# One more preparation step ahead of layer 0's expert tiles, early row loads, and two sine products moved from GpSimd to VectorE

## The chip, the core and the metric

The kernel runs on one core of a Trainium2 chip. A core has TensorE (PE in the rows; PEld is its weight load), VectorE (DVE), ScalarE (ACT), GpSimd (POOL) and SyncE (SP), each with an instruction queue of its own that runs in order; they wait for each other by semaphores. SyncE does nothing here but issue DMAs. The metric is device microseconds of one execution.

## What is computed

Two layers over a batch of 8 rows (sequences) of 512 tokens with 128 channels. The change is in layer 0, between its first mixing part and its attention scores. Cut to what matters there:

```
xn = layernorm(x)
# attention of layer 0, its preparation per batch row
q_amp = softplus(xn @ Wq_amp.T);  k_amp likewise      # then divided by the head's root mean square
q_phi = pi * tanh(xn @ Wq_phi.T); k_phi likewise
q_cos, q_sin = q_amp * cos(q_phi), q_amp * sin(q_phi) # the same for k
v = xn @ Wv.T
scores = (q_cos . k_cos + q_sin . k_sin) / sqrt(8) * exp(score_log_scale), causal, softmax
# feed-forward of layer 0, after its own small attention y = layernorm(...)
idx = argmax(y @ Wg.T)                                # one of 8 experts per token
out = relu(y @ W1[idx] + b1[idx]) @ W2[idx] + b2[idx]
z = layernorm(y + out) * g2 + be2
```

## The kernel before

The phases setup, mix0, middle0, attend0, middle1, experts1 and attend1 follow each other, each with its own block per engine and a barrier between. The change is in middle0 alone, which does two things side by side.

**Preparation of the attention, one batch row u (0 to 7) after the other.** Row u's 512 x 128 input comes by `load_row`, TensorE transposes it (`turn_row`) and multiplies it with the value, phase and amplitude weights (`values`, `phases`, `amplitudes`, `mean_squares`). ScalarE makes tanh, the softplus out of Abs, Exp and Ln, the sine and the cosine, and the inverse root mean square. VectorE makes |tanh| (`absolute_turn`), the amplitude, its normalised form (`normalise`) and the product with the cosine (`cosine_products`), GpSimd the product with the sine (`sine_products`). VectorE then splits the values into two float16 parts (`split`: a cast and a subtraction), and SyncE stores them to memory as six stacks (`store_stacks`).

**Experts.** At the start VectorE chooses each token's expert (`route_choice`), and GpSimd scatters all 4096 token rows to `sorted0` by expert with 32 indirect DMAs (`scatter`). There are 23 tiles of 256 sorted rows, each with one expert. For tile n SyncE loads the expert's weights and the rows (`load_weights`, `load_rows`; ring of 4 tiles), TensorE transposes the rows (`turn_rows`), projects them in (`into_hidden`) and out (`out_of_hidden`), ScalarE and VectorE each make half of the hidden layer (`half_hidden`), VectorE adds and normalises, GpSimd adds the bias, makes the inverse deviation and applies gain and shift.

What sets the order is one list. A step t has three parts, and each part holds one tile slot, n = 3t + part - FIRST_TILE, with FIRST_TILE = 9; so tiles 0 to 2 are in step 3, and tile 22 is in step 10. Each engine walks this list and does in each part first or last what is due of rows t, t - 1, t - 2 or t - 3 and of tiles n + 1 to n - 3. In step t, TensorE projects row t, ScalarE and VectorE make the amplitude of row t - 1 and normalise row t - 2, and part 0 splits row t - 3. Ahead of the list SyncE loads rows 0 and 1 of the input, waits for the tile table, loads the weights of tiles 0 to 3, then rows 2 and 3, waits until the scatter has landed, and loads the sorted rows of tiles 0 to 3. In the list it stores stacks of row t - 3 and loads row t + 1 in part 0, and loads tile n + 3 in every part. When tile 19 is due it stores the table of the tokens' places, element by element, in eight DMAs (`turn_places`), and when tile 21 is due it waits for these and reads the table back; results of tiles follow in the same queue (`store_result`). GpSimd's queue begins with the scatter, so whatever it does for rows or tiles is behind it.

## Time and profile before

| | us |
|---|---|
| median of 3 runs | 1249.08 |
| lowest and highest of them | 1247.53, 1249.44 |
| the profiled execution, whole | 1250.84 |
| its span in the trace | 1249.3 |
| of that, busy: PE / DVE / ACT / POOL | 990.1 / 835.6 / 680.5 / 638.6 |

The span is that of one execution under the hardware profiler, and the rows further down are from it. A row of a timeline has the start and the duration in microseconds, the engine, the kernel line, the operation, what it writes and reads, how many instructions were merged into it, and in brackets how long the engine had idled before it and what ended that wait. SPq is SyncE's queue issuing a DMA. A row of windows gives each engine's busy time in a stretch, with the number of its instructions, the granted TensorE clock as a share of full speed, the mean busy share of the 16 DMA engines and their GB/s. Layer 0's middle0 lies between about 162 and 387 us.

### The profile page before, as it was taken

What the parts mean: (1) busy time and instruction counts of PE and PEld (TensorE: products, weight loads), DVE (VectorE), ACT (ScalarE), POOL (GpSimd) and SP (SyncE); (2) the same over time, 40 slices, a digit from 0 to 9 for tenths busy, and PEclk for the clock granted to TensorE, in tenths of its full rate; (3) what the DMA queues carried; (4) which work ended last, traced back from release to release, by engine and by line L of the source; (5) the groups of instructions that cost most, each with busy time, mean ns of one, the idle gap of its engine ahead of it and who ended that gap; (6) DMA issues with size and microseconds to landing.
All of it is one profiled execution on the core that took longest, in us unless ns stands there. A gap on an engine that the chain in (4) does not pass through costs nothing. (4 is left out here: it accounts for less than half of the span.)

```text
span 1249.3 us, 25988 instructions
## 1 busy us (share of the span) xinstructions
PE 990.1 (79%) x8908; PEld 647.7 (52%) x8908; DVE 835.6 (67%) x1829; ACT 680.5 (54%) x1293; POOL 638.6 (51%) x908
## 2 busy tenths in 40 slices
PE   3789753989873999999975463499999599999997
PEld 1456431767662555555533342388888245545553
DVE  1566341799986999999937566033333799999992
ACT  1356443777720777777765353122222377777775
POOL 3467537478764454444533456111110467777775
PEclk9899776899996899999997566699999599999999
DMA  4322032477795222222202233466664112211211
GB/s 136 109 50 53 27 101 85 139 212 204 221 144 124 71 78 73 71 70 70 70 8 57 70 109 103 139 191 183 190 193 139 43 43 53 54 53 54 54 47 32
DMA packets 151526, 122.58 MB, mean 98 GB/s; under 512 B 31712, under 2 KB 134032, under 8 KB 151408
## 3 DMA queue, kind: packets, MB, share of 16 engines
q1 hardware_dynamic: 141664, 102.89, 30.2%
q0 software_dynamic: 8016, 17.71, 5.0%
q8 instruction: 67, 1.10, 0.4%
q10 hardware_dynamic: 1728, 0.46, 0.2%
q14 instruction: 51, 0.42, 0.1%
HBM read 75.75 MB, written 42.61 MB: 95 GB/s over the span
## 5 line engine op out<-in xcount | busy, mean ns | idle before, releaser
L2104 ACT ACTIVATE attend_probs<-attend_attend_ps 128x512 f32<-128x512 f32 x640 | 353.8, 601 | 155.3 <-PE attend_attend_ps L2172 144.2
L2071 POOL TENSOR_SCALAR_AFFINE_SELECT attend_probs<-attend_probs 128x512 f32<-128x512 f32 x256 | 159.7, 636 | 194.1 <-ACT attend_probs L2104 193.4
L2172 PE MATMUL attend_attend_ps<-attend_q,attend_ks 50*128 50x512 f16 (+3 forms) x1024 | 235.8, 306 | 22.9 <-ACT attend_probs L2104 20.3
L2140 PE MATMUL attend_attend_ps<-attend_ks,attend_q 48*128 48x512 f16 (+3 forms) x1024 | 191.1, 316 | 30.5 <-DMA attend_ks<-k_stack 22.9
L2185 PE MATMUL attend_attend_ps<-attend_probs,attend_vals 128*32 128x512 f32 (+3 forms) x2048 | 178.3, 445 | 0.0
L2267 DVE TENSOR_REDUCE attend_neg_max<-attend_attend_ps 128x2 f32<-128x1024 f32 x128 | 155.7, 1216 | 13.4 <-PE attend_attend_ps L2152 12.7
L2152 PE MATMUL attend_attend_ps<-identb,stairs 64*128 64x128 bf16 (+1 forms) x1280 | 144.3, 213 | 0.0
L2172 PEld LDWEIGHTS attend_attend_ps<-attend_q,attend_ks 50*128 50x128 f16 x1024 | 70.4, 94 | 119.3 <-ACT attend_probs L2104 72.6
L2269 DVE TENSOR_REDUCE attend_neg_max<-attend_attend_ps 128x2 f32<-128x768 f32 x128 | 121.9, 953 | 7.7 <-PE attend_attend_ps L2152 6.9
L2152 PEld LDWEIGHTS attend_attend_ps<-identb,stairs 64*128 64x128 bf16 x1280 | 104.0, 100 | 19.5 <-issue 4.7
L1887 PE MATMUL experts_experts_ps<-experts_rowsT,experts_w_in 128*128 128x256 f32 (+1 forms) x468 | 110.6, 387 | 1.6 <-ACT experts_rowsT L1836 1.5
L1852 DVE TENSOR_TENSOR experts_hidden<-experts_experts_ps,experts_gate 128x512 f32<-128x512 f32 x39 | 27.0, 692 | 120.7 <-ACT experts_gate L1828 120.7
L1815 POOL DMA_DIRECT2D experts_rows<-sorted x39 | 27.7, 711 | 136.6 <-issue 136.6
L1091 POOL DMA_INDIRECT sorted<-middle_scaled,rank_row x64 | 65.3, 1020 | 59.9 <-issue 38.1
L1887 PEld LDWEIGHTS experts_experts_ps<-experts_rowsT,experts_w_in 128*128 128x128 f32 (+1 forms) x468 | 82.8, 183 | 17.9 <-ACT experts_rowsT L1836 2.1
L2140 PEld LDWEIGHTS attend_attend_ps<-attend_ks,attend_q 48*128 48x128 f16 x1024 | 68.2, 96 | 44.4 <-DMA attend_ks<-k_stack 23.3
L1828 ACT ACTIVATE experts_gate<-experts_experts_ps 128x512 f32<-128x512 f32 x39 | 23.3, 597 | 121.4 <-PE experts_experts_ps L1887 121.4
L2264 DVE TENSOR_REDUCE attend_neg_max<-attend_attend_ps 128x4 f32<-128x1024 f32 x64 | 78.4, 1225 | 9.5 <-PE attend_attend_ps L2152 9.1
L2087 POOL DMA_INDIRECT attend_moe<-done,back_row x64 | 62.1, 970 | 14.9 <-issue 14.9
L1899 PE MATMUL experts_experts_ps<-experts_w_out,experts_hidden 128*128 128x128 f32 (+1 forms) x468 | 58.7, 275 | 0.9 <-DVE experts_result L1863 0.9
L2185 PEld LDWEIGHTS attend_attend_ps<-attend_probs,attend_vals 128*32 128x32 f32 x2048 | 44.7, 108 | 23.9 <-issue 6.4
L1899 PEld LDWEIGHTS experts_experts_ps<-experts_w_out,experts_hidden 128*128 128x128 f32 (+1 forms) x468 | 55.4, 191 | 1.2 <-issue 1.1
(317 smaller groups left out, 1990.4 us busy)
## 6 DMA issues: line engine op xcount, KB each, us to landing
experts_w_in<-in_L_ffn_w_dram SPq DMA_DIRECT2D x78, 176.0 KB, 2.4
q_stack<-middle_parts SPq DMA_DIRECT2D x24, 256.0 KB
k_stack<-middle_parts SPq DMA_DIRECT2D x24, 256.0 KB
attend_q<-q_stack SPq DMA_DIRECT2D x64, 96.0 KB
attend_ks<-k_stack SPq DMA_DIRECT2D x64, 96.0 KB
middle_w_in<-in_L_ffn_W_dram SPq DMA_DIRECT2D x23, 256.0 KB
middle_w_out<-in_L_ffn_W_dram SPq DMA_DIRECT2D x23, 256.0 KB
experts_rows<-sorted POOLq DMA_DIRECT2D x39, 128.0 KB, 2.5
```

The lines of the kernel that those rows point to most:

```text
L1091: pool.indirect_dma_start(k.sorted1, bass.IndirectOffsetOnAxis(ap=k.rank_row[:, c * NT + tile:c * NT + tile + 1], axis=0), scaled[:, c, ti ...
L1887: mm = pe.matmul(ps[0:size[c], hidden_bank(u, bank), half * ROWS:(half + 1) * ROWS], w_in[:, u.phase, w + c * P:w + c * P + size[c]], rows ...
L1899: mm = pe.matmul(ps[:, OUT, a * D:(a + 1) * D], hidden[0:size[c], u.par, c, a * P:(a + 1) * P], w_out[0:size[c], u.phase, c, :], start=(c ...
L2071: pool.affine_select(out=block_, in_=block_, compare_op=ALU.is_ge, fill=0.0, base=0, pattern=[[0, GH], [1, P]], channel_multiplier=-1).the ...
L2104: act.activation(probs[:, u.par, 2 * c + side, :], ps[:, PROB + side, :], ACT.Exp, scale=SCALE ** -2)\
L2140: pe.matmul(ps[:, bank + side, col:col + (qt + 1) * P], q[rows(side, KR), g, pair, qt * P:(qt + 1) * P], ks[rows(side, KR), g, pair, 0:(qt ...
L2152: mm = pe.matmul(span[:, :, col:col + 64], k.stairs[here, stair:stair + P], k.identb[here, here].unsqueeze(1).broadcast_to([64, len(blocks ...
L2172: mm = pe.matmul(ps[:, PROB + side, col:col + S - kt * P], ks[rows(side, KM), g, pair, kt * P:(kt + 1) * P], q[rows(side, KM), g, pair, kt ...
L2185: mm = pe.matmul(ps[32 * h:32 * h + 32, MIX, kt * P:S], vals[:, u.par, kt * GH + h, :], probs[:, u.par, 2 * c + h % 2, col:col + S - kt * ...
L2264: ins = dve.tensor_reduce(out[:, :, :, 1], pair_banks.rearrange("p s (h t) -> p s h t", h=HP), X_AXIS, ALU.max, negate=True)
L2267: ins = dve.tensor_reduce(out[:, :, c // 2, 3], pair_banks, X_AXIS, ALU.max, negate=True)
L2269: dve.tensor_reduce(out[:, :, c // 2, 2], pair_banks[:, :, 0:384], X_AXIS, ALU.max, negate=True)
```

## The change

FIRST_TILE becomes 12, so that each tile meets the row work of one step later, and step 3 has row work and no tile. SyncE's start is written anew: rows 0, 1 and 2 of the input are loaded first, row 3 behind the weights of tile 0, then the weights of tiles 1 to 3. The wait for the scatter and the loads of the first four tiles' sorted rows move into the list, to part 1 of step 3, behind the stacks of row 0 and the load of row 4. The sine products of rows 0 and 1 (rows below EARLY = 2) are made by VectorE, behind its cosine products; those of rows 2 to 7 stay with GpSimd, and wait for the previous row's sine product too.

```
-    FIRST_TILE = 3 * PARTS_OF_STEP
+    FIRST_TILE = 4 * PARTS_OF_STEP
+
+    EARLY = FIRST_TILE // PARTS_OF_STEP - 2
...
-            load_row(0)
-            load_row(1)
+            for u in range(3):
+                load_row(u)
             sp.wait_ge(routing.tiles_ready.sem, 1)
-            for n in range(RING):
+            load_weights(0)
+            load_row(3)
+            for n in range(1, RING):
                 load_weights(n)
-            load_row(2)
-            load_row(3)
-            for done in k.scattered[0]:
-                sp.wait_ge(done.sem, NT // 4 * 16)
-            for n in range(RING):
-                load_rows(n)
             for t, part, n in order:
                 if part == 0:
                     if row(t - 3):
                         store_stacks(t - 3)
                     if t >= 3 and row(t + 1):
                         load_row(t + 1)
+                if n == -2:
+                    for done in k.scattered[0]:
+                        sp.wait_ge(done.sem, NT // 4 * 16)
+                    for first in range(RING):
+                        load_rows(first)
                 if n >= 1 and tile(n + 3):
...
             def sine_products(u):
                 pool.wait_ge(amp_n_done.sem, amp_n_done.done(u))
                 pool.wait_ge(sine_done.sem, sine_done.done(u))
-                if u >= 1:
-                    pool.wait_ge(low_done.sem, low_done.done(u - 1))
+                pool.wait_ge(low_done.sem, low_done.done(u - 1))
+                pool.wait_ge(sine_vals.sem, sine_vals.done(u - 1))
...
-                if part == 1 and row(t - 2):
+                if part == 1 and row(t - 2) and t - 2 >= EARLY:
                     sine_products(t - 2)
...
+            def sine_products(u):
+                dve.wait_ge(sine_done.sem, sine_done.done(u))
+                dve.tensor_tensor(vals[:, :, 1, :], amp_n[:, :, :], sine[:, u % 2, :, :], ALU.mult).then_inc(sine_vals.sem, 1)
...
                 if part == 2 and row(t - 2):
                     cosine_products(t - 2)
+                    if t - 2 < EARLY:
+                        sine_products(t - 2)
```

SyncE's queue between the weights of tile 3 and those of tile 4, before (middle_xn is the input of a batch row, middle_rows the sorted rows of tiles, q_stack and k_stack the stored parts):

```order
L1357 DMA middle_b_out<-in_L_ffn_b_dram 128x128
L1345 DMA middle_xn<-xn 128x4x128 x2
L1361 DMA middle_rows<-sorted 128x2x128 x4
L1381 DMA q_stack<-middle_parts 16x8x1024 x3
L1381 DMA k_stack<-middle_parts 16x8x1024 x3
L1345 DMA middle_xn<-xn 128x4x128
L1352 TENSOR_LOAD tile_expert
```

and now:

```order
L1359 DMA middle_b_out<-in_L_ffn_b_dram 128x128
L1383 DMA q_stack<-middle_parts 16x8x1024 x3
L1383 DMA k_stack<-middle_parts 16x8x1024 x3
L1347 DMA middle_xn<-xn 128x4x128
L1363 DMA middle_rows<-sorted 128x2x128 x4
L1383 DMA q_stack<-middle_parts 16x8x1024 x3
L1383 DMA k_stack<-middle_parts 16x8x1024 x3
L1347 DMA middle_xn<-xn 128x4x128
L1354 TENSOR_LOAD tile_expert
```

The stacks of one row and one more input load now stand ahead of the sorted rows of tiles 0 to 3, and the loads of rows 2 and 3 are gone from here to the front.

VectorE's queue from |tanh| of row 1 to the split of row 0, before (x_sum is the buffer lent for amplitudes and values):

```order
L1653 SCALAR_TENSOR_TENSOR middle_turn_abs<-middle_turn 128x1024 [waits middle0_cosine_done,middle0_tanh_done]
L1690 COPY v_all<-middle_ps 128x512 [waits middle0_v_proj]
L1660 SCALAR_TENSOR_TENSOR x_sum<-middle_ps,middle_logs 128x1024 [waits middle0_log_done]
L1667 TENSOR_TENSOR middle_amp_n<-x_sum,middle_inv 128x1024 [waits middle0_inv_done]
L1674 TENSOR_TENSOR x_sum<-middle_amp_n,middle_cosine 128x2x512 [waits middle0_cosine_done,middle0_amp_n_done]
L1653 SCALAR_TENSOR_TENSOR middle_turn_abs<-middle_turn 128x1024 [waits middle0_cosine_done,middle0_tanh_done]
L1697 TENSOR_SCALAR middle_hidden<-middle_ps,middle_b_in 128x256 [waits middle0_hidden_ps]
L1697 TENSOR_SCALAR middle_hidden<-middle_ps,middle_b_in 128x256
L1684 CAST middle_parts<-x_sum 128x2x1024 [waits middle0_cosine_vals,middle0_sine_vals]
```

and now:

```order
L1656 SCALAR_TENSOR_TENSOR middle_turn_abs<-middle_turn 128x1024 [waits middle0_cosine_done,middle0_tanh_done]
L1697 COPY v_all<-middle_ps 128x512 [waits middle0_v_proj]
L1663 SCALAR_TENSOR_TENSOR x_sum<-middle_ps,middle_logs 128x1024 [waits middle0_log_done]
L1670 TENSOR_TENSOR middle_amp_n<-x_sum,middle_inv 128x1024 [waits middle0_inv_done]
L1677 TENSOR_TENSOR x_sum<-middle_amp_n,middle_cosine 128x2x512 [waits middle0_cosine_done,middle0_amp_n_done]
L1681 TENSOR_TENSOR x_sum<-middle_amp_n,middle_sine 128x2x512 [waits middle0_sine_done]
L1656 SCALAR_TENSOR_TENSOR middle_turn_abs<-middle_turn 128x1024 [waits middle0_cosine_done,middle0_tanh_done]
L1691 CAST middle_parts<-x_sum 128x2x1024 [waits middle0_cosine_vals,middle0_sine_vals]
```

The sine product is new behind the cosine product, and the split of row 0 no longer has tile 0's half of the hidden layer ahead of it.

SyncE's queue at the end of middle0, from the sorted rows of the last tile, before:

```order
L1361 DMA middle_rows<-sorted 128x2x128
L1372 DMA places<-rank_row 16x32x1 x8
L1366 DMA done<-middle_result 128x2x128 x2
L1381 DMA q_stack<-middle_parts 16x8x1024 x3
L1381 DMA k_stack<-middle_parts 16x8x1024 x3
L1408 DMA rank_row<-places 128x32x1
L1366 DMA done<-middle_result 128x2x128 x5
```

and now:

```order
L1363 DMA middle_rows<-sorted 128x2x128
L1374 DMA places<-rank_row 16x32x1 x8
L1368 DMA done<-middle_result 128x2x128 x2
L1411 DMA rank_row<-places 128x32x1
L1368 DMA done<-middle_result 128x2x128 x5
```

The stacks of the last row, which stood between the places and the table read back, now stand ahead of the last two tiles' weights.

## Rows read from the trace of the kernel before

**Rows 1.** Windows: from the start of middle0 to the loads of the sorted rows.
```profile
162.00:217.40 55.40, 27.30 (x68) 14.13 (x68) 17.31 (x34) 23.43 (x23) 33.55 (x33) 0.68 0.34 100
```

**Rows 2.** The scatter's line (ns min/median/max, first and last start), then the timeline of its surroundings.
```profile
L855 POOL DMA_INDIRECT sorted<-y_all,rank_row x32: 954/958/1775, 174.4 to 215.1; - x32
...
190.10 0.93 SPq L1345 DMA_DIRECT2D middle_xn<-xn  x2
...
217.40 1.90 SPq L1361 DMA_DIRECT2D middle_rows<-sorted  x4
...
219.60 0.69 PE L1605 MATMUL middle_ps<-ident,middle_rows 128*128 128x128 f32 x2 [5.47 <-DMA middle_rows<-sorted]
```

**Rows 3.** Timeline, single rows of the preparation: ScalarE, TensorE, VectorE, GpSimd.
```profile
185.91 1.00 ACT L1472 ACTIVATE middle_turn<-middle_ps 128x1024 f32<-128x1024 f32 x1
...
194.31 0.58 ACT L1479 COPY middle_xnT<-middle_ps 128x512 f32<-128x512 f32 x1 [7.41 <-issue]
...
203.58 1.13 ACT L1512 ACTIVATE middle_cosine<-middle_turn_abs,col 128x1024 f32<-128x1024 f32 x1
...
197.48 1.64 PE L1575 MATMUL middle_ps<-wT,middle_xnT 128*128 128x128 f32 x8
...
208.47 0.69 DVE L1690 COPY v_all<-middle_ps 128x512 f32<-128x512 f32 x1 [20.31 <-remote]
...
211.46 1.23 DVE L1674 TENSOR_TENSOR x_sum<-middle_amp_n,middle_cosine 128x1024 f32<-128x1024 f32 x1
...
216.06 2.36 POOL L1425 TENSOR_TENSOR x_sum<-middle_amp_n,middle_sine 128x1024 f32<-128x1024 f32 x1
```

**Rows 4.** Windows, one per step of three tiles, from tile 0's half on VectorE.
```profile
224.76:243.78 19.02, 18.16 (x91) 14.52 (x90) 15.76 (x26) 15.68 (x22) 5.88 (x5) 0.97 0.49 139
243.78:265.14 21.36, 19.05 (x105) 15.35 (x103) 20.25 (x36) 15.40 (x22) 16.27 (x17) 1.00 0.72 203
265.14:286.36 21.22, 19.04 (x105) 15.35 (x103) 20.24 (x36) 15.40 (x22) 16.27 (x17) 1.00 0.76 207
286.36:306.84 20.48, 19.08 (x105) 15.38 (x103) 20.15 (x35) 15.45 (x22) 16.28 (x17) 1.00 0.75 214
306.84:327.32 20.48, 19.57 (x103) 15.42 (x102) 20.15 (x35) 15.91 (x24) 16.28 (x17) 1.00 0.73 212
327.32:346.39 19.07, 15.18 (x81) 13.57 (x80) 18.52 (x33) 13.27 (x18) 15.46 (x17) 0.91 0.72 209
346.39:367.54 21.15, 16.01 (x84) 13.77 (x82) 17.95 (x32) 6.97 (x13) 16.12 (x18) 0.92 0.84 189
367.54:386.22 18.68, 8.22 (x58) 7.45 (x56) 14.24 (x29) 1.93 (x5) 12.13 (x19) 0.91 1.18 124
```

**Rows 5.** Timeline, the sixth step: split, stacks, next weights, next tile's rows.
```profile
328.11 1.22 DVE L1684 CAST middle_parts<-x_sum 128x2048 f16<-128x2048 f32 x1
...
332.65 1.90 SPq L1381 DMA_DIRECT2D k_stack<-middle_parts  x3
...
336.03 0.36 SPq L1353 DMA_DIRECT2D middle_w_in<-in_L_ffn_W_dram  x1
...
341.37 0.44 PE L1605 MATMUL middle_ps<-ident,middle_rows 128*128 128x128 f32 x2 [0.91 <-DMA middle_rows<-sorted]
```

**Rows 6.** Timeline, the seventh step: TensorE turns the rows of tile 21; outputs.
```profile
361.03 0.44 PE L1605 MATMUL middle_ps<-ident,middle_rows 128*128 128x128 f32 x2 [2.99 <-DMA middle_rows<-sorted]
362.02 3.29 PE L1627 MATMUL middle_ps<-middle_w_out,middle_hidden 128*128 128x128 f32 x16 [0.55 <-DVE middle_hidden L1697]
```

**Rows 7.** Timeline, the last step and its end: SyncE, TensorE, GpSimd.
```profile
362.13 4.74 SPq L1372 DMA_DIRECT2D places<-rank_row  x8
...
379.08 0.36 SPq L1408 DMA_DIRECT2D rank_row<-places  x1
...
373.82 2.02 PE L1627 MATMUL middle_ps<-middle_w_out,middle_hidden 128*128 128x128 f32 x16 [1.04 <-DVE middle_second L1703]
...
385.50 0.72 POOL L1450 TENSOR_TENSOR middle_result<-middle_gained,row 128x256 f32<-128x256 f32 x1 [0.16 <-DMA done<-middle_result]
```

## The prediction, made before the changed kernel had run

> **What bounds the kernel now.** I first read the stretch between the end of layer 0's mixing stage and the first expert tile, as one window. Of its 55.40 us VectorE is busy for 17.31, ScalarE for 23.43 and TensorE for 27.30, while GpSimd issues the scatter [rows 1]. The scatter is 32 indirect DMAs of 0.958 us, started from 174.4 to 215.1 [rows 2]. The four loads of sorted rows go out at 217.40, when the scatter has landed, and TensorE turns the first rows at 219.60, after waiting for that DMA [rows 2]. So the scatter sets where the tiles start, and what stands beside it has slack. In that slack rows 0 and 1 and part of row 2 of the attention preparation are done today; the input of row 2 is issued only at 190.10, behind the weights of four tiles [rows 2].
>
> From there on the question is what sets a step, that is three tiles and one batch row. I cut the stretch at VectorE's first half of the hidden layer of tiles 0, 3, 6 and so on up to the last GpSimd operation of tile 22 (which begins at 385.50 and takes 0.72) [rows 4, 7]. The reader should see eight windows, S1 to S8, of 19.02, 21.36, 21.22, 20.48, 20.48, 19.07, 21.15 and 18.68 us, together 161.46. VectorE is busy for 20.15 to 20.25 in S2 to S5, which looks like a VectorE bound. But S7 contradicts it: VectorE has 17.95 us there, and the step is longer than S4 and S5 [rows 4].
>
> What sets S6 and S7 is a loop through SyncE. In S6: VectorE's split of row 5 starts at 328.11; SyncE can then store the six stacks, the last of which leave by 332.65 + 1.90 = 334.55; only then does it come to the next tile's weights, at 336.03; the tile's last load lands when TensorE turns its rows at 341.37, having waited 0.91 for the DMA [rows 5]. TensorE's output of tile 16 and its projection of tile 18 follow, VectorE's half at 346.39 starts the next step, and the next split comes 0.8 behind it. In S7 the same loop runs again: TensorE waits 2.99 for tile 21's load at 361.03, and the output after it takes 3.29, where 16 such matmuls took 2.02 at the high clock (2.4 GHz) in the last step [rows 6, 7] (the granted clock of S7 is 0.92, of S6 0.91, of S2 to S5 1.00) [rows 4, 6]. So full steps are bound by VectorE and this loop nearly together, and a step with less VectorE work is bound by the loop alone, at 19.1 to 21.2 us.
>
> **The change, part by part.**
>
> *One step more of preparation before the tiles.* Tiles keep their 23 slots, but every tile meets the row work of one step later. Before: S1 to S5 carry all of a row's work, S6 and S7 less and less, S8 the last split. After: a step without tiles lies under the scatter; S1' to S4' carry full row work, S5' that of S6, S6' that of S7, S7' only the last split and its stacks, S8' none. Rows 5, 6 and 7 are loaded in S1' to S3'. So S1' is like S1 (19.02: the first step, both with a row load), S2' and S3' like the three full steps with a row load (mean of 21.36, 21.22, 20.48: 21.02), S4' like S5 (20.48), S5' like S6 (19.07) [rows 4]. One 21.02 step is gone, and a step S7' with split and three tiles is new.
>
> *S6' and S7'.* Both still have the split, six stacks and a load behind them, hence the loop. S6 and S7 measured it as 19.07 and 21.15 [rows 4]; I take the mean, 20.1, for each, since nothing says on which side the clock and the load fall. Bounds: 19.07 and 21.15 for the loop; below it, for VectorE alone, 17.95 for S6' (its work is S7's) and 17.95 less a normalisation and a cosine product of about 1.23 each, 15.5, for S7' [rows 3, 4].
>
> *S8'.* It is S8 without the split. In S8 TensorE's output of tile 21 starts at 373.82, having waited 1.04 for VectorE's sum of tile 20, which stood behind the split [rows 7]; that wait goes, and some 0.4 more in the next sum. 18.68 less 1.4 is 17.3; bounds 18.68 (the end is held by DMAs, below) and 15.9 (twice the saving).
>
> *The sum of the tiles' part.* 19.02 + 2 x 21.02 + 20.48 + 19.07 + 20.1 + 20.1 + 17.3 = 158.1, against 161.46: 3.4 us less.
>
> *Row loads ahead of the weights.* Row 2's load waits only for the turn of row 0 and goes out some 20 us before 190.10; row 3's waits for row 1's turn and stands behind one tile's weights instead of four. This makes room for the extra step. ScalarE, which has the most work in it, is done with tanh of row 1 at 186.91; from its copy of row 2 at 194.31 to the end of row 1's cosine it needed 203.58 + 1.13 - 194.31 = 10.4 us [rows 3], and with a square and a tanh of about 1.0 each the period of a row is 12.4. So ScalarE is through row 2's copy to row 1's cosine at about 197.4, and through the next row's at about 210, before 217.40. The split of row 0 comes at about 201 on VectorE (behind tanh of row 2), and its six stacks are issued by about 209, so SyncE is back at its wait for the scatter before the scatter ends. Price on the start of the tiles: 0, with 7 us to spare. The four first tiles' weights move back by one or two DMA issues and aren't read before 219.60.
>
> *Sine products of rows 0 and 1 on VectorE.* GpSimd's took 2.36 at 216.06, after the scatter, because its queue is in order; VectorE needs about 1.23 (the cosine product of the same size) [rows 3]. On VectorE they lie under the scatter. Without this move the split of row 0, and with it SyncE's stacks and the row loads queued behind them, would wait for the scatter. Price 0; if the cover were gone it would be 2.5 us on VectorE. GpSimd loses one product before tile 0 (its next work, the bias of tile 0, needs the rows that TensorE too waits for) and one in the first step. Its two waits in the other products are older than what they wait for: 0.
>
> *Waits moved.* SyncE's wait for the scatter now stands behind the stacks of row 0 and the load of row 4. Queued behind it are the four row loads, for which TensorE and GpSimd wait. What the stacks and that load still have in the DMA rings at 217.4 goes ahead of tile 0's rows: I say 0, at most 2 us. A further price from the first tile's matmuls at low clock isn't changed, as TensorE idles ahead of them in both.
>
> The Trainium skill, SBUF — State Buffer, section "SBUF: two separate sides", says that a VectorE copy or cast in a two-port mode locks GpSimd out of writing the descriptors of its own DMAs. The split's cast (1.22 us, [rows 5]) newly lies beside the scatter; by the rule the scatter and the first tile come up to 1.2 us later, and the time would be 1246.9. The trace has no such cast beside a scatter; the longest of the 32 issues is 1.775 us where the usual one is 0.958 [rows 2]. My sum goes by 0.
>
> **Total.** The profiled execution has a span of 1249.3 and took 1250.84; the median of the runs is 1249.08, and I subtract from that: 1249.08 - 3.4 = 1245.7.
>
> **Rivals.**
>
> *The end is held by DMAs (1249).* The eight stores of places go out at 362.13, 15 us behind the split that opens S7; SyncE gets past its wait for them at 379.08, and behind that wait stands the store of tile 18, for which GpSimd's last result waits at 385.50 (0.16 us) [rows 7]. From the opening split to the end that is 39.0 us however short S8' gets. After the change the stacks of row 7 no longer stand in the rings behind the places, which speaks for an earlier landing. If it doesn't help, S7' and S8' together stay at 39.8, and with S6' at 20.1 the gain is 1.0: 1248.1; with S6' at 21.15 it is 0: 1249.
>
> *VectorE sets the steps after all (1239).* Then S6', S7' and S8' take 18.0, 15.5 and 17.3 instead of S4 to S8's 21.02, 21.15 and 18.68: 10.0 less. For it: busy 20.2 of 20.5 in S4 and S5. Against it: S7.
>
> *The preparation outlasts the scatter (slower).* TensorE's values of row 2 end at 197.48 + 1.64 = 199.1 in the records, but VectorE's copy of them starts at 208.47, and the profile names no engine for that wait of 20.31 [rows 3]. This lateness of 9.4 us is hidden today. Once more of it in the longer preparation uses up the 7 us and lets TensorE's last projection of row 3 end at about 220; that still costs nothing much. If it strikes each of rows 2 and 3, the first tile starts 9 us later: 1245.7 + 9 = 1255. It decides from more than 7 us of such lateness on, and costs from about 10.
>
> *The change doesn't do what it says:* the order on each engine shows it does; what is left is that the extra step isn't under the scatter, which is the rival above.
>
> **How the numbers follow.** Chances: the loop, with a gain of 1.5 to 6, 0.56; end held by DMAs, or S6' at its longest, 0.24; VectorE-bound 0.13; preparation too long 0.07. The likeliest one gives 1245.7. The range is 1241.5 to 1249.5: it takes in the loop's bounds (both new steps at 19.07 and S8' at 15.9 would be 6.8 less, 1242.3) and the DMA-held end, and leaves out most of the two outer cases. 0.2% is 2.5 us, about what a measurement of this kernel can tell from no change. Faster by more needs a gain of 2.5: 0.47 of the first case and all of the third, 0.60. Slower by more 0.07. The rest, 0.33, is the same.
>
> **What would show it.** Row 2 turned by about 186 and the extra step's ScalarE work done by 212; row loads still at 217.4 and the first turn at 219.6; the opening split of the last two full steps 19 to 21 us apart with TensorE waiting for the row DMA near their end; GpSimd's last result 36 to 37 us behind the split of row 7. Wrong would be: a first turn after 221 (start), a step with split and less VectorE work shorter than 18.5 (then VectorE was the bound), or the last split to end at 39 again (then the places).

## The result

The changed kernel took 1262.8 us (median of 4 runs, 1252.7 to 1268.0) against 1249.3 for the kernel before: a ratio of 1.0098, 95% interval 1.0056 to 1.0140. Predicted were 1245.7 and a range of 1241.5 to 1249.5. In this comparison it is slower, and in its first trace by the mechanism to which I had given 0.07.

One fact belongs beside every number below. The kernel before stood at two levels in six comparisons: medians of 1249.3, 1252.5, 1251.8 and 1247.7 in four of them, 1225.3 and 1223.5 in two (one chip was at both levels). I call them the upper and the lower level. At the upper one the changed kernel measured 1.0098 and later 1.0023 (0.9982 to 1.0063), at the lower one 0.9993 (0.9972 to 1.0014); neither of the later two can be told from no change. Where the levels differ is the main finding of the experiments.

The timeline of the changed kernel's preparation, VectorE and ScalarE (start, duration, in brackets the idle time before and who ended it):

```profile
202.44 0.69 DVE L1697 COPY v_all<-middle_ps 128x512 f32<-128x512 f32 x1 [13.93 <-remote]
...
214.44 1.22 DVE L1691 CAST middle_parts<-x_sum 128x2048 f16<-128x2048 f32 x1
215.70 2.29 DVE L1693 TENSOR_TENSOR middle_parts<-x_sum,middle_parts 128x2048 f16<-128x2048 f32 x1
...
196.41 1.13 ACT L1515 ACTIVATE middle_cosine<-middle_turn_abs,col 128x1024 f32<-128x1024 f32 x1
...
212.24 1.02 ACT L1475 ACTIVATE middle_turn<-middle_ps 128x1024 f32<-128x1024 f32 x1 [6.89 <-remote]
221.06 0.58 ACT L1482 COPY middle_xnT<-middle_ps 128x512 f32<-128x512 f32 x1 [7.79 <-remote]
```

The same stretch on TensorE, GpSimd and SyncE:

```profile
185.12 0.60 PE L1572 MATMUL middle_ps<-ident,middle_xn 128*128 128x128 f32 x4
...
189.19 1.05 PE L1578 MATMUL middle_ps<-wT,middle_xnT 128*128 128x128 f32 x8
...
207.89 1.06 PE L1572 MATMUL middle_ps<-ident,middle_xn 128*128 128x128 f32 x4
...
231.41 0.38 PE L1608 MATMUL middle_ps<-ident,middle_rows 128*128 128x128 f32 x2
...
214.11 1.67 POOL L855 DMA_INDIRECT sorted<-y_all,rank_row  x1 [0.30 <-issue]
216.08 2.73 POOL L855 DMA_INDIRECT sorted<-y_all,rank_row  x1 [0.30 <-issue]
...
215.69 2.84 SPq L1383 DMA_DIRECT2D q_stack<-middle_parts  x3
...
221.62 2.44 SPq L1363 DMA_DIRECT2D middle_rows<-sorted  x4
```

Row 2 was turned at 185.12 and row 1's cosine done at 197.54, as forecast (186 and 197.4). Then the preparation stands still three times. By the records the values of row 2 end at 190.24 on TensorE, and VectorE copies them at 202.44. ScalarE's tanh of row 2 starts at 212.24, though the phases end at 194.25. (The brackets say "remote" where no record of an instruction or a DMA ends near the semaphore's update; below this is a wait without a releaser, and what it waited for a late result.) Row 3 is turned by 208.95 and copied at 221.06. So the preparation lasts until 231.4, and the first turn of sorted rows is at 231.41 without a wait for a DMA, 11.8 us later than before [rows 2]. The split of row 0 slipped from a forecast 201 to 214.44, and the stacks and row loads with it.

The eight steps of three tiles, as [rows 4] for the kernel before (length, then busy time of TensorE with its count, weight loads, VectorE, ScalarE, GpSimd, granted clock, DMA share, GB/s):

```profile
235.25:253.43 18.18, 16.76 (x85) 13.19 (x84) 15.59 (x27) 14.86 (x21) 5.89 (x5) 1.00 0.51 147
253.43:273.90 20.47, 19.42 (x106) 15.71 (x105) 20.14 (x35) 15.77 (x23) 16.28 (x17) 1.00 0.78 211
...
314.86:336.37 21.51, 16.66 (x81) 14.32 (x81) 18.61 (x34) 13.37 (x19) 16.67 (x19) 0.84 0.70 193
336.37:357.17 20.80, 15.99 (x84) 13.66 (x82) 16.77 (x32) 6.86 (x13) 12.94 (x17) 0.92 0.71 199
357.17:378.83 21.66, 14.45 (x78) 13.02 (x76) 12.83 (x29) 3.52 (x9) 9.39 (x15) 0.92 0.71 177
378.83:398.55 19.72, 9.69 (x58) 8.68 (x58) 10.04 (x27) 2.05 (x5) 11.53 (x19) 0.87 0.58 41
```

Together they are 163.30 (S3' and S4' are 20.48 each), where I forecast 158.1 and the kernel before had 161.46. The span, 1259.5 against 1249.3, is these 1.8 more and 10.5 at the start (235.25 against 224.76), less 2.1 behind the experts. The first four are together shorter than forecast by 1.9, the last four longer by 7.1. S7' has only 12.83 us of VectorE work and still lasts 21.66.

### The profile page after: what moved, and what is told of

It is laid out like the page before. It is cut to its first block and busy times, and to the rows that moved or that the text cites. A ratio compares the mean times of both kernels' runs of the same rounds, so it can differ in the third digit from the quotient of the medians.

```text
span 1259.5 us, 25992 instructions
## 1 busy us (share of the span) xinstructions
PE 1001.8 (80%) x8908; PEld 654.6 (52%) x8908; DVE 833.8 (66%) x1831; ACT 680.8 (54%) x1293; POOL 628.1 (50%) x906
## 5 line engine op out<-in xcount | busy, mean ns | idle before, releaser
L1896 PEld LDWEIGHTS experts_experts_ps<-experts_rowsT,experts_w_in 128*128 128x128 f32 (+1 forms) x468 | 82.5, 183 | 17.7 <-ACT experts_rowsT L1845 2.1
L2273 DVE TENSOR_REDUCE attend_neg_max<-attend_attend_ps 128x4 f32<-128x1024 f32 x64 | 78.4, 1225 | 10.9 <-PE attend_attend_ps L2161 10.7
L1630 PE MATMUL middle_ps<-middle_w_out,middle_hidden 128*128 128x128 f32 x368 | 50.7, 296 | 8.0 <-ACT middle_rowsT L1536 6.8
```

What stands on the lines that cost most here:

```text
L1896: mm = pe.matmul(ps[0:size[c], hidden_bank(u, bank), half * ROWS:(half + 1) * ROWS], w_in[:, u.phase, w + c * P:w + c * P + size[c]], rows ...
L2273: ins = dve.tensor_reduce(out[:, :, :, 1], pair_banks.rearrange("p s (h t) -> p s h t", h=HP), X_AXIS, ALU.max, negate=True)
```

## What makes TensorE's results late

My first theory, A: results of TensorE reach the other engines late while GpSimd's indirect scatter is in flight. Against it, B: the weights' transfers beside the preparation do it. C: it is TensorE's own idleness.

**The scatter held back.**

```
+            pool.wait_ge(projected.sem, projected.done(3))
             scatter(pool, k)
```

> The changed kernel, with GpSimd's scatter held back until TensorE's amplitudes of row 3; the weights of four tiles are still loaded beside rows 1 to 3. Theory A (TensorE's results reach the other engines late only while GpSimd's scatter is in flight): with no scatter beside it the preparation runs without late results; VectorE's copy of row 2's values starts within 2 us of the end of the values on TensorE (12.2 us behind it in the changed kernel) and amplitudes of row 3 end by 212, against 231.4. The scatter (44 us) then sets the start: sorted-row loads near 250, first turn near 253, time 1262 + 21 = about 1283. Theory B (the weights' transfers cause it) and theory C (TensorE itself, at its low clock and mostly idle): the late results are still there, amplitudes of row 3 end at about 230, sorted rows are loaded near 275, time about 1305.

It took 1284.2. VectorE, SyncE and TensorE in the timeline of that kernel:

```profile
189.18 0.69 DVE L1698 COPY v_all<-middle_ps 128x512 f32<-128x512 f32 x1 [2.87 <-PE middle_ps L1579]
...
251.07 1.92 SPq L1363 DMA_DIRECT2D middle_rows<-sorted  x4
...
253.11 0.69 PE L1609 MATMUL middle_ps<-ident,middle_rows 128*128 128x128 f32 x2 [44.66 <-DMA middle_rows<-sorted]
```

No result was late in layer 0, amplitudes of row 3 ended at 208.5, row loads and time came as A had them. The same kernel at the lower level:

> The changed kernel with the scatter held back until amplitudes of row 3, again. Theory A: no result of TensorE over 3 us late between 172 and the scatter's start, amplitudes of row 3 end by 212, scatter of 40 us behind it; and where the other traces of this call have late results, this one has them in layer 1 too. If the clean stretch of the first run was chance, one of three or so results is late by 5 to 12 us again.

It took 1255.5, with its first turn at 256.27. So in layer 0, where no scatter stood beside the preparation, the lower level brought nothing; from the end of layer 0's experts to the end of the program it was 832.2 against 862.6. In this pair the whole difference of the levels lies there, behind layer 0's experts.

**The weights moved behind the scatter** (tiles 0 to 3, each ahead of its rows):

```
-            load_weights(0)
             load_row(3)
-            for n in range(1, RING):
-                load_weights(n)
...
                     for first in range(RING):
+                        load_weights(first)
                         load_rows(first)
```

> The changed kernel, with the weights of the first four tiles loaded only behind SyncE's wait for the scatter, each ahead of its rows. Theory A: the late results stay, VectorE's copy of row 2's values at about 202, first turn a little later than 231.4 since tile 0's weights too leave only at 221; time 1262 to 1268. Theory B: the late results are gone, the preparation ends by 212, the split of row 0 runs at about 201 and SyncE stands at its wait for the scatter before 217; first turn at 224 to 228 behind the weights, time 1254 to 1258. Theory C: as A.

It took 1254.6, as B expected, with one late result (ScalarE waited 3.63 us for row 3's turn) and VectorE's copy of row 2's values at 190.59. The preparation ended at 213.9 and the first turn came at 227.71, behind tile 0's weights. Taken alone this speaks for B. But a third trace of the changed kernel as it is, below, has none in that stretch either, with the weights there; one trace can't tell.

**Plain DMAs instead of indirect ones** (tokens stay unsorted, so the experts see other rows):

```
-        pool.indirect_dma_start(k.sorted0, bass.IndirectOffsetOnAxis(ap=k.rank_row[:, t:t + 1], axis=0), k.y[:, t, :], None)\
+        pool.dma_start(k.sorted0[t * P:(t + 1) * P, :], k.y[:, t, :])\
```

> The changed kernel, with the 32 indirect DMAs of the scatter replaced by 32 plain GpSimd DMAs of the same 128 rows, written in the order of the tokens (so the sorting of the rows is left out and the experts see other rows). Theory A in its narrow form (it is the indirect DMA's descriptor work on GpSimd): the late results are gone, amplitudes of row 3 end by 212, and since the plain DMAs are all issued by about 200 the preparation sets the start: first turn 205 to 213, time 1243 to 1252. Theory A in its wide form (any DMA by GpSimd) and theory C: late results stay, first turn 220 to 231.

It took 1253.4, with its first turn at 214.53 (wait 3.13 us for the rows), nothing late in layer 0, although the weights were loaded beside it. The time was not won: in layer 1, whose scatter is still indirect, the copy of the logits was late three times (11.61, 11.58 and 6.80 us), and that scatter took 111.8 us from its first to its last issue, against 97.5 to 106.2 in the other ten traces at this level whose layer 1 scatter is indirect.

**TensorE kept busy.** Ten matmuls behind row 2's phases:

```
                     phases(t)
+                    if t == 2:
+                        pe.wait_ge(routing.tiles_ready.sem, 1)
+                        for _ in range(10):
+                            pe.matmul(ps[:, HID0, :], k.wT[:, W_QP, :], xnT[:, :], start=True, stop=True)
```

> The changed kernel, with ten more matmuls of 128x512 on TensorE behind row 2's phases, into a bank that nothing reads at that time: TensorE, which stood idle for 10.06 us there, is busy for about 9.3 us more, until some 203.5. Theory A (results are late while indirect scatter DMAs are in flight, whatever TensorE does): VectorE's copy of row 2's values still starts 7 to 12 us behind their end at about 190. Theory C (results are late only when TensorE falls idle behind them while a scatter is in flight): the copy starts within 2 us of 190 and tanh of row 2 at about 198; then amplitudes of row 2 come at 204 behind the extra matmuls, and late results can still follow those. Time: A 1261 to 1268; C 1255 to 1262.

That run took 1221.7 on the lower level, with nothing late in it or its three neighbours. Again, at the upper level:

> The changed kernel with ten more matmuls behind row 2's phases, again: the first run of it fell where no result was late in any of four kernels, so that it told nothing. If results are late now in the other kernels: theory A puts VectorE's copy of row 2's values 7 to 12 us behind their end here too; theory C (only when TensorE falls idle) within 2 us. If they are late in none of the four, it tells nothing again: first turn 221.0.

It took 1258.8. TensorE and VectorE in its timeline:

```profile
194.75 8.75 PE L1650 MATMUL middle_ps<-middle_xnT,wT 128*128 128x512 f32 x20
...
202.44 0.69 DVE L1701 COPY v_all<-middle_ps 128x512 f32<-128x512 f32 x1 [13.27 <-remote]
```

TensorE is busy until 203.5, the copy is as late as without that (values end at 190.91). C falls, by this one trace.

**The changed kernel twice more.**

> The changed kernel itself, unchanged, once more and on the chip of the two kernels before: for a second trace of it, and its time beside theirs. Theory A: at least one result of TensorE in the scatter's 44 us arrives over 3 us late again, not by the same amounts or in the same places; first turn anywhere from 222 (one of them, hidden) to 232; median 8 to 14 us above the kernel before. If the first trace was an odd execution, first turn by 222 and a time within 4 us of the kernel before.

> The changed kernel, unchanged, for a third trace and time. Where TensorE's results aren't late, as in its second trace: first turn 220.2, eight steps 159.7, time 0 to 3 us below the kernel before. Where they are: first turn 222 to 232, and the time 3 to 13 us above the kernel before of the same comparison.

The first of the two (lower level, 1223.6 against 1225.3) had nothing late and its first turn at 220.22. The second (upper level, 1256.0 against 1251.8) had nothing late in layer 0, first turn at 225.19, but was late in layer 1. So at the upper level it varies in layer 0 from trace to trace: of ten with the indirect scatter beside the preparation, nine have semaphores of TensorE updated over 5 us behind the recorded ends, and eight of them one to three waits without a releaser. The kernel before has it too and doesn't pay:

> The kernel before, unchanged, for a trace beside those of this call. The kernel before took 1249 to 1252 in two of the comparisons and 1225 in a third, in which the four kernels' traces show no late result of TensorE at all. If that is what sets the two levels, this trace either shows no wait that the profile puts down to nobody, a stretch behind layer 0's experts of about 834, and 1219 to 1228, or it shows them beside both scatters, that stretch at 859 to 865, and 1245 to 1255. First turn 219.6 to 220.3 in either case, eight steps 161.5, or 1 to 1.5 less.

It took 1251.6, at the upper level, with one wait of 17.43 us without a releaser in layer 0, its first turn at 220.07, and 861.2 behind layer 0's experts. Its eight steps took 163.23, where its first trace had 161.46.

**Layer 1.** There the scatter is 64 indirect DMAs beside the next rows' routing. ScalarE's copy of turned rows, one per batch row, in the changed kernel's first trace:

```profile
713.33 0.59 ACT L1123 COPY middle_xnT<-middle_ps 128x512 f32<-128x512 f32 x1 [3.08 <-remote]
726.84 0.58 ACT L1123 COPY middle_xnT<-middle_ps 128x512 f32<-128x512 f32 x1 [3.06 <-remote]
740.10 0.58 ACT L1123 COPY middle_xnT<-middle_ps 128x512 f32<-128x512 f32 x1 [3.05 <-remote]
```

and in its second, at the lower level:

```profile
702.25 0.59 ACT L1123 COPY middle_xnT<-middle_ps 128x512 f32<-128x512 f32 x1
712.48 0.59 ACT L1123 COPY middle_xnT<-middle_ps 128x512 f32<-128x512 f32 x1
722.71 0.59 ACT L1123 COPY middle_xnT<-middle_ps 128x512 f32<-128x512 f32 x1
```

A row takes 13.3 us in one and 10.2 in the other. The test is that scatter made plain:

```
-                    pool.indirect_dma_start(k.sorted1, bass.IndirectOffsetOnAxis(...), scaled[:, c, tile, :], None)
+                    at = (c * NT + tile) * P
+                    pool.dma_start(k.aside[at:at + P, :], scaled[:, c, tile, :])
```

> The changed kernel, with the 64 indirect DMAs of layer 1's scatter replaced by plain GpSimd DMAs of the same rows into a tensor that nothing reads (layer 1's experts then work on zeros, which 17 more stores of 1 MB put there early in the program; they may lengthen the first 170 us). To be read in the stretch from the end of layer 0's experts to the end of the program alone: 859 to 864 where results were late, 833 to 837 where none was. Theory A: no wait without a releaser in layer 1, and that stretch at 825 to 838 whatever layer 0 shows. If the two levels have another cause (a slower engine or memory), it stays near 860 where the others are at 860.

It fell on the lower level (828.9 behind layer 0's experts, nothing late) and was repeated:

> As the first run with plain DMAs in place of layer 1's scatter. It tells something only if the kernel before takes some 1250 in this comparison. Then theory A: no wait without a releaser after 450 us, and a stretch from the end of layer 0's experts to the end of 827 to 835, where the changed kernel took 861 to 864 at that level. If the level has another cause, 855 to 865.

Now the kernel before took 1247.7. VectorE and ScalarE in layer 0, where the scatter is still indirect, and then in layer 1:

```profile
234.30 0.69 DVE L1698 COPY v_all<-middle_ps 128x512 f32<-128x512 f32 x1 [9.39 <-remote]
...
245.01 0.59 ACT L1483 COPY middle_xnT<-middle_ps 128x512 f32<-128x512 f32 x1 [4.76 <-remote]
...
731.39 0.58 ACT L1124 COPY middle_xnT<-middle_ps 128x512 f32<-128x512 f32 x1
741.54 0.58 ACT L1124 COPY middle_xnT<-middle_ps 128x512 f32<-128x512 f32 x1
751.76 0.58 ACT L1124 COPY middle_xnT<-middle_ps 128x512 f32<-128x512 f32 x1
```

In one and the same execution TensorE's results are late beside the indirect scatter and not one is late beside the plain one; a row takes 10.2 us, and the stretch behind layer 0's experts is 834.7, where the changed kernel took 861.0 and 863.6 at that level. As a whole this kernel took 1258.9 in the first run, at the lower level, and 1258.0 in the second, at the upper one; 828.9 against 834.7 of it lie behind layer 0's experts, and ahead of that point the first run was the longer one (428.4 against 421.7). That is shown, then, by one execution: at the upper level TensorE's results come late beside an indirect scatter, by 1.6 to 18 us behind the end that the records give, and not beside plain DMAs. A plain DMA also writes its 128 rows to one block where the scatter spreads them; which of the two matters, no run tells apart. Over the 20 traces: the twelve at the upper level have 3 to 15 waits without a releaser each, every one for TensorE and beside an indirect scatter; the eight at the lower level have none.

The levels differ in a second place. Layer 1's attention issues eight indirect DMAs per batch row that gather rows. Its first issues of two following rows, in the run with plain DMAs at the upper level,

```profile
1059.94 0.99 POOL L2097 DMA_INDIRECT attend_moe<-done,back_row  x1 [0.16 <-issue]
1091.09 0.99 POOL L2097 DMA_INDIRECT attend_moe<-done,back_row  x1 [0.15 <-issue]
```

and at the lower:

```profile
1063.36 0.99 POOL L2097 DMA_INDIRECT attend_moe<-done,back_row  x1 [0.16 <-issue]
1093.82 0.99 POOL L2097 DMA_INDIRECT attend_moe<-done,back_row  x1 [0.16 <-issue]
```

A row takes 31.15 us in one and 30.46 in the other. Averaged over six rows it is 31.1 to 31.4 in all twelve traces at the upper level and 30.46 in all eight at the lower, while the inner rows of layer 0's attention, which gathers with four such DMAs a row, take 30.1 in all twenty. No wait there lacks a releaser, and no run changes the gathers, so a cause isn't shown. Of the some 25 us between the levels the stretch of layer 1's scatter makes the larger part (82.5 to 84.2 us from first to last issue at the lower level), some 4 follow between its last issue and layer 1's experts, and about 2 to 8 are the attention's. Why the level is the upper one in some comparisons and not in others, and whether the weights' transfers make late results more frequent in layer 0, stays open.

## What the scatter pays for VectorE beside it

GpSimd's line of the scatter (ns min/median/max, first and last start): changed kernel, third trace,

```profile
L855 POOL DMA_INDIRECT sorted<-y_all,rank_row x32: 957/962/2737, 175.3 to 220.7; - x32
```

and with the sine products of rows 0 and 1 on GpSimd again (`EARLY = 0`), which keeps those products and the split of row 0 out of the scatter:

```profile
L855 POOL DMA_INDIRECT sorted<-y_all,rank_row x32: 957/962/1776, 172.2 to 212.5; - x32
```

> The changed kernel with the sine products of rows 0 and 1 back on GpSimd, behind the scatter. I said that without that move the split of row 0, and with it SyncE's six stacks and the row loads behind them, would wait for the scatter. Then GpSimd's product runs from 216 to 218.4, the split to 222, the stacks are issued by 227.5, the sorted rows go out at 228 and the first turn is at 235 (their landing behind the stacks), 15 us later than the 220.2 of the changed kernel without late results; time about 1238 where that takes 1223. A theory in which the stacks don't matter to the row loads has the first turn by 223.

It took 1262.8 with three late results, and its preparation, not the rows, set the first turn at 229.14; so the 235 is not tested. The scatter is: 40.3 us from first to last start, against 45.4. The kernel before has 40.7 [rows 2], and five traces of kernels without that VectorE work beside it lie between 40.3 and 41.0, eight with it between 43.7 and 45.4. (The changed kernel's first trace has 41.3, because its split came only at 214.44; its last issue then took 2.73 us.) VectorE and GpSimd in the third trace of the changed kernel show where it goes:

```profile
201.15 1.22 DVE L1691 CAST middle_parts<-x_sum 128x2048 f16<-128x2048 f32 x1
202.41 2.29 DVE L1693 TENSOR_TENSOR middle_parts<-x_sum,middle_parts 128x2048 f16<-128x2048 f32 x1
...
207.00 1.22 DVE L1670 TENSOR_TENSOR middle_amp_n<-x_sum,middle_inv 128x1024 f32<-128x1024 f32 x1
...
209.39 1.22 DVE L1681 TENSOR_TENSOR x_sum<-middle_amp_n,middle_sine 128x1024 f32<-128x1024 f32 x1
...
201.00 1.50 POOL L855 DMA_INDIRECT sorted<-y_all,rank_row  x1 [0.30 <-issue]
202.80 2.74 POOL L855 DMA_INDIRECT sorted<-y_all,rank_row  x1 [0.30 <-issue]
205.84 0.96 POOL L855 DMA_INDIRECT sorted<-y_all,rank_row  x1 [0.30 <-issue]
207.10 1.94 POOL L855 DMA_INDIRECT sorted<-y_all,rank_row  x1 [0.30 <-issue]
209.35 0.96 POOL L855 DMA_INDIRECT sorted<-y_all,rank_row  x1 [0.30 <-issue]
```

An issue of 0.96 us takes 1.50 beside row 2's |tanh| and the cast, 2.74 beside the subtraction, 1.94 beside the product that normalises row 1. It is mainly the operation already running when an issue starts that counts: over the 17 traces with an indirect scatter and no stores of places beside it, the first issue of each left aside, the 20 issues that started under a normalising product, and the 9 under the subtraction, all ended 0.83 us behind it. The sine products start just behind an issue, and all 16 beside the scatter in those traces left theirs at 0.95 to 0.96. So did 31 issues under VectorE's amplitude operation, which reads one of its two inputs from PSUM. The rule of the Trainium skill (SBUF — State Buffer, section "SBUF: two separate sides") is that a VectorE operation in a two-port mode, or one with two inputs from SBUF beside a GpSimd operation that reads SBUF, and the GpSimd operation exclude each other, and the one that starts first goes through. The trace agrees with it; I had weighed it for the cast alone, at 1.2 us, and left it out of the sum. Measured it is 3 to 5 us: 1.8 are the subtraction's, about 0.5 the cast's with the |tanh| ahead of it, the rest falls where an issue happened to start under another |tanh| or a normalising product. The trace before could have warned me: its longest issue, 1.775 us [rows 2], started under a |tanh|.

The products on GpSimd aren't free either. The split then waits for the product behind the scatter,

```profile
213.59 2.36 POOL L1428 TENSOR_TENSOR x_sum<-middle_amp_n,middle_sine 128x1024 f32<-128x1024 f32 x1
...
215.98 1.23 DVE L1691 CAST middle_parts<-x_sum 128x2048 f16<-128x2048 f32 x1 [3.24 <-POOL x_sum L1428]
```

and SyncE's row loads left 50.6 us behind the scatter's start, against 46.0 and 47.7 in the two traces of the changed kernel without late results in layer 0, and 43.0 before.

## What the extra step and the early rows are worth alone

**The early rows alone** (first tile at its old place, sine products on GpSimd):

```
-    FIRST_TILE = 4 * PARTS_OF_STEP
+    FIRST_TILE = 3 * PARTS_OF_STEP
-    EARLY = FIRST_TILE // PARTS_OF_STEP - 2
+    EARLY = 0
```

> Only one part of the change: rows 1 to 3 of the preparation loaded ahead of the tiles' weights, with the first tile at its old place and all sine products on GpSimd. All theories: the first turn stays at 219.6 since the preparation needed before tile 0 is the old one; time as before within 2.5 us (1247 to 1251). If the early row loads themselves cost (through the weights that now come later) it would be 2 us or more slower.

The ratio to the kernel before is 1.0003 (0.9963 to 1.0044), first turn at 220.21, eight steps 161.56. It had a late result of 8.85 us in layer 0 and TensorE still waited 17.11 for the sorted rows: with the old depth there is slack for it.

**The loads of the next tile ahead of the stacks,** on the kernel before and on the changed one:

```
+                if n >= 1 and tile(n + 3):
+                    load_weights(n + 3)
+                    load_rows(n + 3)
                 if part == 0:
                     if row(t - 3):
                         store_stacks(t - 3)
...
-                if n >= 1 and tile(n + 3):
-                    load_weights(n + 3)
-                    load_rows(n + 3)
```

> The kernel before, with SyncE's six stores of the stacks (5.2 us of issue) moved behind the loads of the next tile in the first part of each step. If the loop through SyncE (split, six stacks, next tile's loads, their landing, TensorE) sets the last steps, as I read them, the waits of TensorE for the rows' DMA (0.91, 2.99 us) and of the sums behind them go: S6 and S7, 19.07 and 21.15, fall to about 18.5 and 18.0, that is 2 to 4 us less than the kernel before. If the steps are set by something else (clock, VectorE), the time is the same within 1.5.

> The changed kernel with the same move. There the loop stands in three steps, S5' to S7' of 21.51, 20.80 and 21.66 us, with TensorE waiting 3.39, 4.22 and 2.26 us for the rows' DMA. Loop theory: S5' to S8' (83.7 together) fall to 72 to 76, the time by 7 to 11 us against the changed kernel. If the slow steps come from the granted clock (0.84 to 0.92) and not from the loads, 0 to 3 us less.

On the kernel before: 1220.4 against 1225.3, ratio 0.9976 (0.9955 to 0.9997). It is the one version here below both kernels, if barely. Its S6 and S7 were 18.76 and 19.73, S8 20.90 (19.07, 21.15 and 18.68 in [rows 4], a trace at the other level). On the changed kernel: 1223.5, no different from the changed kernel's 1223.6 beside it. Windows of the last three steps of the latter without the move, at the same level,

```profile
324.07:345.59 21.52, 16.00 (x84) 13.86 (x82) 17.94 (x32) 6.97 (x13) 15.84 (x18) 0.92 0.68 194
345.59:368.30 22.71, 15.80 (x80) 14.01 (x78) 13.02 (x29) 3.53 (x10) 12.93 (x18) 0.85 0.88 177
368.30:384.60 16.30, 7.98 (x58) 7.45 (x56) 10.07 (x27) 1.94 (x5) 10.50 (x17) 0.90 0.59 50
```

and with it:

```profile
328.95:347.51 18.56, 14.48 (x81) 12.16 (x79) 17.75 (x34) 6.98 (x13) 15.14 (x16) 1.00 0.72 213
347.51:364.43 16.92, 13.05 (x78) 11.79 (x78) 13.46 (x31) 3.35 (x9) 12.38 (x17) 1.00 0.79 222
364.43:389.20 24.77, 10.71 (x58) 9.71 (x58) 10.27 (x27) 2.05 (x5) 11.53 (x19) 0.75 0.76 49
```

The loop through SyncE is real: without the stacks ahead of the loads S6' and S7' are 8.8 us shorter. But 8.5 of it come back in the last step, where TensorE waits 6.06 us for the last tile's rows, which were issued behind the stacks of row 7 and right ahead of the places, and then runs at a granted clock of 0.50 (1.2 GHz) until about 376 us (0.75 in the step's mean).

**The places moved away from the end.** Under the scatter (`turn_places()` behind the last early load, both with the loads ahead):

> The kernel before with the next tile's loads ahead of the stacks, and the eight stores of places moved from tile 19 to under the scatter, behind the load of row 3. If the end of the experts is held by the places and by what stands in the DMA rings with them, the last step falls from 18.7 to 20.9 to about 16.3, and the time is 3 to 6 us below the kernel before. If it is held by the last tile's load behind the stacks, 1 to 3 us below.

> The changed kernel with both moves. With the loads ahead of the stacks alone its steps S6' and S7' were 18.56 and 16.92 and the last one 24.77, with TensorE waiting 6.06 us for the last tile's rows. Places theory: the last step falls to 16.3 to 18, the eight steps to 151 to 153 against 159.4; the time is 6 to 9 us below the changed kernel. Stacks theory: the wait stays at 4 us or more and the eight steps at 157 or more.

The ratios to the kernel before are 1.0045 (1.0018 to 1.0072) and 1.0041 (1.0016 to 1.0066). The eight steps did fall, to 158.25 and 156.46, and the last one to 18.46 and 21.76, 2.4 and 3.0 less than with the loads ahead alone, so that much of the end is the places'; the rest of TensorE's wait there, 3.04 of 6.06, is not. But the scatter stretched to 52.0 and 54.6 us. One store behind the loads of each of tiles 4 to 11:

```
-                if n == TL - RING:
-                    turn_places()
+                if 4 <= n < 4 + B:
+                    turn_places([n - 4])
```

> The kernel before with the next tile's loads ahead of the stacks and one store of places behind the loads of each of tiles 4 to 11, instead of all eight behind those of tile 19. First turn as in the kernel before. If the places hold the end: the last step, 20.89 with the loads ahead alone, falls to 18.5 as with the places under the scatter, the eight steps from 160.2 to about 158, the time 4 to 6 us below the kernel before (ratio 0.995 to 0.997). If each store of places delays the loads behind it in the steps where it now stands, the first five steps grow by 1 to 3 us in all and nothing is won (0.998).

The ratio is 1.0187 (1.0135 to 1.0239): the third to fifth steps became 23.61, 30.78 and 32.09. The last one, 20.43, hardly gained. The places cost least where they stood.

## Why the prediction was wrong

- *Price on the start of the tiles: 0, with 7 us to spare.* This step failed, in two terms. I counted one lateness of 9.4 us as what might strike and needed two for a cost; in the first trace there were three in a row, each standing ahead of the next in the chain of copy, tanh and the next copy, so that the preparation and not the scatter set the first turn, 11.8 us later. The second term is the scatter's own length, which would have cost even without them. Measured from its start, the first turn is at 45.2 before (44.7 to 45.6 in four like kernels), 56.7 in the first trace of the changed kernel, and 48.2 and 49.9 in those without late results: 3 to 5 us are what the scatter costs alone, 7 to 8.5 what the late results add to it. The third rival named the mechanism, and its 1255 was on the right side of the 1262.8; its chance of 0.07 was far too small, since at the upper level nine of ten traces have late results in layer 0. The wait "<-remote" of 20.31 us [rows 3] stood in the trace, and I let it count as noise because it was hidden there, while the change took away just what hid it.
- *Sine products on VectorE: price 0.* So it was for the products themselves: none lengthened an issue of the scatter. But the split that they let run under it did, and with an |tanh| and the normalising products it makes the scatter 3 to 5 us longer. That is the cast which my sum took at 0, and the subtraction behind it, which I hadn't weighed at all.
- *Row loads ahead of the weights; ScalarE through the extra step by 210; the loads of the sorted rows at 217.4.* The first came as said (row 2 turned at 185.12). Without late results the preparation ended at 209.1 in the third trace, so the chain was costed rightly. The row loads left at 221.62 in the first trace, behind the stacks of the late split, and 46.0 and 47.7 us behind the scatter's start without late results, against 43.0.
- *Waits moved: 0, at most 2.* Right where nothing is late: the stacks were issued by 207.7 in the third trace, long before the scatter's end.
- *The tiles' part: -3.4.* Against the 161.46 of [rows 4] it was -1.7 and -1.5 without late results in front (159.74 and 160.00), +1.8 in the first trace. But the kernel before isn't steady there: its second trace has 163.23, and against that, in one comparison, the third trace of the changed kernel is 3.2 less. S2' and S3', forecast at 21.0, took 20.5 to 20.9; S6' and S7' at 20.1 were the mis-sized term: 20.8 to 21.5 and 21.7 to 22.8; S8', forecast at 17.3, took 16.3 and 15.8, and 19.7 in the first trace. S7' and S8' together: 39.0 and 38.6, 41.4 in the first trace, where I forecast 37.4. That is nearer to the rival of an end held by DMAs, which had 39.8; the moves of loads and places show its two parts, the last tile's load behind the stacks (the larger) and the places (2.4 to 3.0).
- Total: without late results +3 to 5 at the start and -1.5 to -3.2 in the tiles. In the comparison at the upper level that has a trace of each, the span of the changed kernel is 3.8 us longer (1253.8 against 1250.0): 4.6 at the start, -3.2 in the tiles, 2.4 behind the experts, where the edit changes nothing. For the 0.9993 at the lower level no trace of the unchanged kernel before stands beside it, so how it adds up stays open. At the upper level the late results come on top, in most executions but not in all.

## What to carry to other kernels

A wait to which the profile gives no releaser may be hidden today and yet real; before the slack that hides it is used up, count how often it could strike in the longer chain, and look at several traces. Work under a scatter by GpSimd is not free even if no engine is shared: an issue that met the cast, or started under an operation with both inputs in SBUF, became longer (up to 2.74 us instead of 0.96). And here a shorter step ahead of the last one gained only what the last load let through: 8.8 us won in two steps, 8.5 lost in the last.

## What I had not expected of the hardware

- The same program stands at two levels, 1223 to 1225 and 1248 to 1253 us, in different comparisons. Most of the difference lies beside GpSimd's indirect scatters: 10.2 or 13.3 us for a batch row of layer 1. Part of the rest is in the attention of layer 1: 30.46 or 31.1 to 31.4 us a row. Indirect DMAs that gather, in both attentions, showed no wait without a releaser in any trace, nor did plain DMAs from GpSimd. So a ratio measured at one level need not hold at the other (here 0.9993 and 1.0098).
- Eight small transposing stores cost the work beside them 9 to 11 us on a scatter, and 3 to 12 us on each of three steps of tiles.
